# Graph attention on one Trainium2 core: the one-hots of the nodes move from VectorE to GpSimd

## The reference, cut to what matters

```python
def _gatv2(x, edge_index, Wl, bl, Wr, br, att, bias):      # h = 3 heads, d = 128
    loops = jnp.arange(n)
    src = jnp.concatenate([edge_index[0], loops])
    dst = jnp.concatenate([edge_index[1], loops])
    xl = (x @ Wl + bl).reshape(n, h, d)
    xr = (x @ Wr + br).reshape(n, h, d)
    e = jax.nn.leaky_relu(xl[src] + xr[dst], NEG_SLOPE)
    score = jnp.einsum('ehd,hd->eh', e, att)
    m = jax.ops.segment_max(score, dst, num_segments=n)
    ex = jnp.exp(score - m[dst])
    denom = jax.ops.segment_sum(ex, dst, num_segments=n)
    alpha = ex / denom[dst]
    out = jax.ops.segment_sum(alpha[:, :, None] * xl[src], dst, num_segments=n)
    return out.reshape(n, h * d) + bias
```

## Time and profile before

| | |
|---|---|
| time, median of 3 runs | 7210.68 us (7207.19 to 7213.8) |
| the profiled execution | 7218.68 us |
| its span, first to last instruction | 7216.6 us |
| VectorE busy | 6002.7 us (83% of the span) |
| TensorE busy | 5244.3 us (73%) |
| GpSimd busy | 3953.3 us (55%) |
| ScalarE busy | 3700.4 us (51%) |
| mean granted TensorE clock | 0.921 of full speed |

### The profile page before, as it was taken

One profiled execution on the slowest core, in us unless ns is written; L12 is line 12 of the kernel. 1 busy time (PEld: TensorE's weight loads), 2 busy tenths in 40 slices (PEclk: granted clock), 3 DMA queues, 4 the chain that ended last, 5 costly groups with the idle time before them and its releaser, 6 DMA issues. The chain is left out here.

```text
span 7216.6 us, 134164 instructions
## 1 busy us (share of the span) xinstructions
PE 5244.3 (73%) x20244; PEld 3043.4 (42%) x20245; DVE 6002.7 (83%) x16763; ACT 3700.4 (51%) x17817; POOL 3953.3 (55%) x3546
## 2 busy tenths in 40 slices
PE   3544444499956889898988789898989846566663
PEld 2444433133323444444445444444444435555552
DVE  9766657799965999999998499999999855777776
ACT  5111113300014999999996399999999831000000
POOL 0688888860002666666662166666666405777773
PEclk9999999899978999999999899999999967777775
DMA  0465664000013555555553255555555404444443
GB/s 11 78 78 79 78 72 50 1 1 0 0 33 125 139 140 140 139 140 139 140 137 64 90 140 140 139 139 138 140 140 139 91 19 120 126 125 125 125 125 68
DMA packets 440612, 705.63 MB, mean 98 GB/s; under 512 B 146470, under 2 KB 315464, under 8 KB 440146
## 3 DMA queue, kind: packets, MB, share of 16 engines
q0 software_dynamic: 185888, 481.62, 26.2%
q1 hardware_dynamic: 254642, 223.19, 15.7%
HBM read 668.31 MB, written 33.88 MB: 97 GB/s over the span
## 5 line engine op out<-in xcount | busy, mean ns | idle before, releaser
L1173 POOL DMA_INDIRECT feat_area<-xl_table,feat_area x1856 | 2002.6, 1079 | 2120.9 <-issue 1196.4
L1324 ACT ACTIVATE feat_area<-feat_area 128x130 f32<-128x130 f32 x5568 | 1644.5, 297 | 216.9 <-DVE feat_area L1377 214.8
L1234 PE MATMUL bank<-node_area,feat_area 128*128 x3712 | 1472.2, 520 | 357.8 <-DVE feat_area L1369 193.9
L1308 ACT ACTIVATE feat_area<-feat_area 128x128 f32<-128x128 f32 x4640 | 1441.8, 387 | 0.0
L1247 PE MATMUL bank<-feat_area 128*128 128x390 f32 x3712 | 1410.6, 503 | 18.0 <-DVE feat_area L1391 4.2
L564 POOL DMA_INDIRECT rec_by_dst<-feat_area,gather_col x800 | 1059.1, 1324 | 248.9 <-issue 223.1
L1736 POOL DMA_INDIRECT feat_area<-kv_table,feat_area x832 | 839.9, 1009 | 561.5 <-DMA feat_area<-gather_src 306.7
L1234 PEld LDWEIGHTS bank<-node_area,feat_area 128*128 128x128 f32 x3712 | 636.2, 191 | 1005.9 <-issue 752.7
L1324 ACT ACTIVATION_READ_ACCUMULATOR feat_area<-feat_area 128x1 f32 x5568 | 1040.3, 187 | 0.0
L1247 PEld LDWEIGHTS bank<-feat_area 128*128 128x128 f32 x3712 | 673.0, 191 | 584.5 <-issue 172.8
L1369 DVE TENSOR_TENSOR feat_area<-bank,feat_area 128x780 f32<-128x780 f32 x928 | 885.8, 955 | 28.6 <-DMA feat_area<-xl_table,feat_area 27.8
(11 more groups left out here) (294 smaller groups left out, 7291.5 us busy)
## 6 DMA issues: line engine op xcount, KB each, us to landing
feat_area<-lo_slot SPq DMA_DIRECT2D x464, 128.0 KB, 3.3
node_area<-in_dst SPq DMA_DIRECT2D x200, 250.0 KB
feat_area<-xl_table,feat_area POOLq DMA_INDIRECT x1856, 3.4
feat_area<-lo_slot_src SPq DMA_DIRECT2D x208, 128.0 KB, 3.3
node_area<-lo_edge SPq DMA_DIRECT2D x200, 125.0 KB
xl_table<-feat_area SPq DMA_DIRECT2D x98, 195.0 KB, 2.2
feat_area<-kv_table,feat_area POOLq DMA_INDIRECT x832
rec_by_dst<-feat_area,gather_col POOLq DMA_INDIRECT x800
```

Source lines behind the costliest of these rows:

```text
L1173: pool.indirect_dma_start(ring[:, at:at + HE], None, k.xl, bass.IndirectOffsetOnAxis(ap=index[s // CG][:, n:n + 1], axis=0)).then_inc(gath ...
L1234: last = nc.tensor.matmul(pair[s % 2][:, u, 0:HE], pick[s // 2 % 2][:, c:c + P], k.node[:, ds(columns[0], HE)], start=True, stop=True)
L1308: last = nc.scalar.activation(row[:, 0:D], row[:, 0:D], ACT.Copy, scale=row[:, D:D + 1])
L1324: last = nc.scalar.activation(at, at, ACT.Copy, accum_out=score[s // CG][:, to:to + 1])
```

## The change

In `gat_edges` the step `places` leaves VectorE's list. GpSimd gets it, behind its gathers in each turn, for group t - 13. It makes the one-hot with one `tensor_scalar` for each of the two tiles, a comparison of `iota_f` with one column as a per-partition scalar. There are now four buffers `place` instead of two, so that it waits for the sums of four groups before. The column comes from a new buffer `lane` for a chunk of 16 tiles, two of them, which SyncE fills from `lo_col` by a DMA once a chunk (new step `load_lanes`, behind a wait on `placed`, lead -4). The work area grows by 520 words a partition. The third attention (`edge_attention`) keeps its own `places` on VectorE.

```diff
--- before.py
+++ after.py
@@ -59,7 +59,7 @@
 SLOPE = 0.2
 
 NODE_W = max((NB + 1) * HE, 2 * NPAD + NB * VW)
-WORK_W = 14200
+WORK_W = 14720
 
 
 class Order:
@@ -1117,15 +1117,17 @@
     nc = k.nc
     groups, U = GROUPS, 2 * CG
     V = 4
+    Q = 4
     W = GS * HE
     cut = Carver(k.wide)
     ring = cut(U * W)
     ring4 = ring.rearrange("p (t h w) -> p t h w", h=H, w=DW)
     z = [cut(W) for _ in range(V)]
     pick = [cut(2 * GS * P) for _ in range(2)]
-    place = [cut(GS * P) for _ in range(2)]
+    place = [cut(GS * P) for _ in range(Q)]
     lo_bc = [cut(GS * P, BF16) for _ in range(2)]
     index = [cut(CT, I32) for _ in range(2)]
+    lane = [cut(CT) for _ in range(2)]
     att_w = cut(HE)
     score = [cut(CR) for _ in range(2)]
     gate = [cut(4 * P, F32, CR) for _ in range(2)]
@@ -1145,7 +1147,8 @@
     by_chunk = lambda v: v.rearrange("o (h t) -> o h t", t=CROW)
 
     gathered = [k.gather_sem(f"a{tag}_gathered{s}") for s in range(U)]
-    index_set, lo_ready, gate_set = ([k.sem(f"a{tag}_{n}{s}") for s in range(2)] for n in ("index", "lo", "gate"))
+    index_set, lo_ready, gate_set, lane_ready = ([k.sem(f"a{tag}_{n}{s}") for s in range(2)]
+                                                 for n in ("index", "lo", "gate", "key"))
     names = ("loaded", "order", "preset", "picked", "looked", "added", "weighed", "reduced", "placed", "weighted",
              "byvec", "summed", "acced", "fixed")
     (loaded, order, preset, picked, looked, added, weighed, reduced, placed, weighted, byvec, summed, acced,
@@ -1174,7 +1177,20 @@
                                             bass.IndirectOffsetOnAxis(ap=index[s // CG][:, n:n + 1], axis=0)
                                             ).then_inc(gathered[s], 16)
 
-            pipeline(pool, groups, [(0, gather)], U)
+            def places(j, s):
+                g = U * j + s
+                if s % CG == 0:
+                    pool.wait_ge(lane_ready[s // CG], 16 * j + 16)
+                if later(g, Q):
+                    pool.wait_ge(summed, g - Q + 1)
+                pool.nop(nofuse=True)
+                for u in range(GS):
+                    n = s % CG * GS + u
+                    last = nc.gpsimd.tensor_scalar(place[s % Q][:, u * P:(u + 1) * P], k.iota_f[:, :],
+                                                   lane[s // CG][:, n:n + 1], None, ALU.is_equal)
+                last.then_inc(placed, 1)
+
+            pipeline(pool, groups, [(0, gather), (-13, places)], U)
 
         @block.sync
         def _(sp):
@@ -1216,7 +1232,16 @@
                         sp.dma_start(rowgate[n][0:1, at:at + CT], k.rowgates[d:d + 1, ds(chunk(j, s) * CT, CT)]
                                      ).then_inc(gate_set[n], 16)
 
-            pipeline(sp, groups, [(12, load_index), (8, load_keys), (0, load_gates)], U)
+            def load_lanes(j, s):
+                if s % CG:
+                    return
+                c = chunk(j, s)
+                if later(c, 2):
+                    sp.wait_ge(placed, (c - 1) * CG)
+                    sp.nop(nofuse=True)
+                sp.dma_start(lane[s // CG], k.lo_col[:, ds(c * CT, CT)]).then_inc(lane_ready[s // CG], 16)
+
+            pipeline(sp, groups, [(12, load_index), (8, load_keys), (0, load_gates), (-4, load_lanes)], U)
 
         @block.tensor
         def _(pe):
@@ -1244,7 +1269,7 @@
                     pe.wait_ge(acced, g - 1)
                 for u in range(GS):
                     at = s * W + u * HE
-                    last = nc.tensor.matmul(sums_in[s % 2], place[s % 2][:, u * P:(u + 1) * P], ring[:, at:at + HE],
+                    last = nc.tensor.matmul(sums_in[s % 2], place[s % Q][:, u * P:(u + 1) * P], ring[:, at:at + HE],
                                             start=u == 0, stop=u == GS - 1)
                 last.then_inc(summed, 1)
 
@@ -1376,12 +1401,6 @@
                 zu = z[s % V].rearrange("p (u e) -> p u e", u=GS)
                 nc.vector.scalar_tensor_tensor(out=zu, in0=zu, scalar=0.0, in1=att_w.unsqueeze(1).to_broadcast([P, GS, HE]),
                                                op0=ALU.max, op1=ALU.mult).then_inc(weighed, 1)
-
-            def places(j, s):
-                g = U * j + s
-                if later(g, 2):
-                    dve.wait_ge(summed, g - 1)
-                key_rows(k, place[s % 2], k.lo_col, g * GS, GS).then_inc(placed, 1)
 
             def weight(j, s):
                 if s % 2:
@@ -1492,7 +1511,7 @@
                 nc.vector.tensor_scalar(fade_col[n], fade_col[n], 1.0, k.stays[:, ds(chunk(j, s) * CG, 1)], ALU.add, ALU.mult
                                         ).then_inc(faded, 1)
 
-            pipeline(dve, groups, [(-13, add_up), (-2, scans), (-3, shift_rows), (1, add), (-2, sequence), (-11, places),
+            pipeline(dve, groups, [(-13, add_up), (-2, scans), (-3, shift_rows), (1, add), (-2, sequence),
                                    (-2, carry), (0, weigh), (-2, spread_fwd), (-3, spread_weights), (-11, weight),
                                    (4, picks), (-2, spread_bwd), (4, first_lane)], U)
```

## The result

The changed kernel takes 8085.03 us (median of 4 runs, 8080.05 to 8089.4), the kernel before 7210.83 us beside it: a ratio of 1.1213, interval 1.1199 to 1.1227. That is 874 us slower, far outside the predicted range. Its profiled execution has a span of 8083.6 us.

The account below looks back on a forecast made before the run. VectorE was taken to bound at 3.43 us a group; without `places`, GpSimd's 3.35 plus 0.03 gives 3.38 us, 46 us gained: 7218.7 - 46 - 8 = 7164 us, own range 7130 to 7195, whole range 7098 to 7400.

Parts of the forecast that it names:

- GpSimd's sum: GpSimd's time a group in the two graph layers: 2.50 + 0.05 + 0.16 + 0.08 + 2 x 0.28 = 3.35 us.
- the price of a comparison: One 128x128 comparison on GpSimd: 0.28 us, from the IOTA's 0.19 plus 0.09 for fetching column and row.
- gathers, with their waiting: GpSimd's two gathers a group, 0.95 us shown each, their waiting for VectorE's `weigh` falling from 0.26 to 0.16 us.
- The far end of my bounds: Upper bound for one comparison on GpSimd: one half of a free slot, 0.45 us, more than twice the IOTA.
- the free slot: GpSimd's time a group left for other work beside its gathers: some 0.9 of 3.43 us.
- Rival 2: GpSimd becomes the bound from 0.32 us a comparison; 7313 us at 0.36, 7480 at 0.45; chance 0.27.
- wrong by mechanism: Signs in the next profile: `weigh`, `weight` or `picks` longer than now, or gathers over 1.08 us on average.
- The first of the two comparisons pays like one gather: On GpSimd, the first comparison of a group waits for VectorE as long as one gather does: 0.08 us.
- A wait of chance arrivals: GpSimd's waiting goes with the square of VectorE's stretch: 1.6 to 1.25 us, so 0.26 to 0.16 us a group.
- Rival 3: Comparisons hold up VectorE's `weigh` or `weight`: 3.66 us a group, 213 us more, 7424 us; chance 0.10.
- ScalarE as the next bound: ScalarE's own work, 3.31 us a group, is the next limit after VectorE; at most 111 us can come back.
- SyncE's part: 116 more small DMAs on SyncE behind a wait on `placed`: put at nothing; uncovered 430 us.

Follow-up runs that it names:

- experiment 3: The change with GpSimd's comparisons replaced by memsets of the same 128x128 words, one-hots left out: 7610.81 us, ratio 0.9918 to the kernel before.
- experiment 7: The change with each comparison covering 64 of the 128 columns, the other half left out: 7792.36 us in one run.
- experiment 5: The change with GpSimd making the one-hots of every fourth group only (3, 7, 11, 15 of 16), VectorE the rest: 7314.98 us, ratio 1.0127 to the kernel before.
- experiment 6: The change with GpSimd making the one-hots of every eighth group only, VectorE the rest: 7242.41 us, ratio 1.0030 to the kernel before.
- experiment 12: Experiment 5 with GpSimd taking groups 2, 6, 10, 14 of 16 instead: 7209.96 us, ratio 0.9997 to the kernel before.
- experiment 4: The change with VectorE's `weigh` given one SBUF input, attention weights left out: 8004.64 us in one run, 326 us over the kernel before on this chip.
- experiment 11: Experiment 5 with GpSimd taking groups 1, 5, 9, 13 of 16 instead: 7226.6 us, ratio 1.0022 to the kernel before.
- experiment 10: Experiment 6 with its comparisons replaced by memsets, these one-hots left out: 7170.72 us, ratio 0.9942 to the kernel before.
- experiment 1: The change with `places` back on VectorE, staged keys, wait and four buffers kept: 7684.85 against 7678.18 us for the kernel before, ratio 1.0012.
- experiment 2: The change with GpSimd comparing into two buffers nobody reads, VectorE making TensorE's one-hots: 8694.6 us in one run, 1016 us over the kernel before.
- experiment 8: The change with each comparison against a constant in place of the staged column, real keys left out: 8009.3 us in one run.

## Why the prediction was wrong

**The terms of GpSimd's sum.** The step that failed is the price of a comparison, "I choose 0.28 us": the shortest take 0.60 us, and the mean in the steady piece is 0.82 us with the waits. In the steady piece of the change:

| us a group | predicted | measured |
|---|---|---|
| two comparisons, unhindered | 0.56 | 1.21 |
| their waiting | 0.08 | 0.42 |
| gathers, with their waiting | 2.06 | 2.27 |
| gaps | 0.65 | 0.50 |
| sum | 3.35 | 4.40 |

The unhindered pair is the 604 ns of the shortest from 2800 to 3800 us, twice; the waiting is what is left of the 1.63 us. Gathers are 721.5 us and gaps 159.9 us for 318.5 groups. Of the error of 1.05 us the bare price is 0.65, the comparisons' waiting 0.34, and the gathers are 0.21 us longer, of which the gaps give 0.15 back. The far end of my bounds, 0.45 us, was no bound either: I had made it from the free slot and the IOTAs, and an instruction that only writes says nothing of one that reads and compares (experiments 3 and 7: 0.19 us against 0.60). The page GPSIMD Engine Reference of the Trainium skill gives 1.8 cycles an element for a tight loop in its "Elementwise — side-by-side cycle accounting", from which I had estimated 0.27 us; the measured 2.5 ns an element and 0.28 us fixed are well above that and above the estimate by its two-input rate, 0.36 us.

**Rival 2, GpSimd becomes the bound, is what happened.** Its signs came: GpSimd waits for nothing, `add` waits for the DMA. Its decision point, 0.32 us a comparison, agrees with the runs, but none came near it: a memset at 0.19 us is on the one side and the comparison at 0.60 on the other. The signs under "wrong by mechanism" came too: `weigh` and `picks` are longer than before, and gathers take 1133 ns on average. Only its size was wrong, since I let it end at 0.45 us: the rival's own formula with 0.60 us and no more waiting gives 2.79 + 1.21 = 4.00 us, 529 us more; the remaining 0.40 us a group is the longer waiting for VectorE, which makes 0.34 in the comparisons and 0.06 in the gathers and gaps.

**The waiting.** "The first of the two comparisons pays like one gather" was wrong: 0.08 us against 0.42, and the second pays too (from 2800 to 3800 us the first of a pair takes 843 ns on average, the second 800). I had the right mechanism from the earlier trace rows and the wrong law for it. A wait of chance arrivals supposes that GpSimd gets in when the instruction that it met is over; in fact it passes over several two-input instructions in a row, up to 3.9 us for a pair (experiment 5). How busy VectorE is doesn't decide it, but what the comparison meets: 820 ns on average in the change with VectorE 73% busy, 1792 ns in experiment 6, where all fall on the chunk's turn, at 98%, but only 835 ns in experiment 12 at 99%. What experiment 4 shows is that `weigh` makes most of it; that the order within VectorE's list decides the rest rests on experiments 5, 6, 11 and 12.

**Rival 3, the comparisons hold up VectorE, is true in a small measure**, and no gather had shown it. In the change it costs VectorE 0.07 us a group (`weigh` 987 against 955 ns, and half of `picks`' 559 against 491) and matters little, as VectorE waits anyway. In experiment 12, where VectorE still bounds, it eats the whole gain. The page SBUF — State Buffer of the Trainium skill says in its section on the shared port pair that the two exclude each other and the later is held whole. Both directions are seen here, but not that order: at 2830.06 `weigh` starts 0.01 us ahead of the comparison, and it is `weigh` that is longer, by 0.25 us and not by the comparison's 0.60; and the comparison of 3017.23 waits for L921 and `weigh`, which start 0.24 and 0.90 us after it and take their usual time (experiment 5).

**What was right.** VectorE's 0.33 us for `places` (experiment 10 gives back an eighth of it, 0.04 us). ScalarE as the next bound at 3.31 to 3.36 us (experiment 3: 3.36). Nothing for SyncE's part, the staging and the four buffers (experiment 1). That the hand-over to TensorE would not count was right as well, though not that it brings no wait: TensorE's `sums` wait 44.3 us of 1400 for a comparison, because GpSimd is late, and experiment 2 is as slow without that. With a write in place of the comparison, two for 0.38 us and nothing read, the kernel is 0.8% faster (experiment 3).

What stays open: why a waiting comparison is passed over by VectorE's next two-input instruction, while a gather at times gets in between; the traces show the durations, not who asked first. That an order of VectorE's list with single-input steps between the others would let comparisons in was not tried; in experiment 5 the single-input steps of 0.15 to 0.22 us between the others did not.

## What to carry to other kernels

- Before an instruction moves to another engine, get its price there from a row of the same operation on that engine. A write of as many elements was three times too cheap as a stand-in, and with 0.9 us of room the price decided the sign.
- Idle time of GpSimd beside a busy VectorE isn't free time. An instruction there that reads SBUF waits for VectorE's two-input instructions (0.42 us a group here) and in turn makes VectorE's longer (0.07 us a group); look at the mean against the median of GpSimd's instructions that are there already, and at what stretch of VectorE's list the new one would meet.
- When a moved step makes a queue the bound, look what else stands in it: here it was of little account that TensorE waited for comparisons; what cost the time is that they made the gathers late, and `add` waited for those.

## What the runs showed of the hardware

- A comparison of 128x128 f32 with a column on GpSimd takes 0.60 us unhindered, 128x64 takes 0.44 us: by these two widths 0.28 us and 2.5 ns an element (experiment 7). With a constant in place of the column it is shown for 0.53 us, but the next still starts 0.60 us after it (experiment 8). Two memsets of the same size take 0.38 us together (experiment 3).
- While VectorE runs two-input instructions back to back, a pair of comparisons was seen to last 3.91 us, and a gather behind it, beside `weigh`, 2.24 us in place of 1.04 (experiment 5). With a one-input `weigh` no comparison in 524 went over 0.91 us (experiment 4).
- A comparison that waits is not let in by the order of starting: VectorE's two-input instructions that started up to 2.6 us after it went ahead of it (experiment 5).
- Behind a comparison the next gather starts after 0.16 us, not the 0.30 us that pass between two gathers, but then takes 1.03 to 1.04 us, not 0.95.
